# Order of the two score matmul pairs within a visit of a fused attention and feed-forward kernel

## What is computed

```python
xn   = layernorm(x)                                  # over the 256 channels
q, k, v = split(xn @ qkv_w + qkv_b)                  # 16 heads of 16 channels
attn = softmax(einsum('bnhd,bmhd->bhnm', q, k) * 0.25)
a    = einsum('bhnm,bmhd->bnhd', attn, v).reshape(b, n, c) @ proj_w + proj_b
h    = silu(xn @ (w_gate/127).T) * (xn @ (w_up/127).T)   # 768 wide
out  = x + a + h @ (w_down/127).T
```

## Time and profile before

| | us |
|---|---|
| three timed runs | 644.5, 646.66, 642.33 (median 644.5) |
| the profiled execution | 647.3 |
| its span in the profile | 645.2 |
| TensorE busy in the span | 608.5 (94%) |
| VectorE busy | 506.7 (79%) |
| ScalarE busy | 365.4 (57%) |
| GpSimd busy | 162.2 (25%) |

### The profile page before, as it was taken

One profiled execution on the slowest core, in us unless ns is written; L12 is line 12 of the kernel. 1 busy time (PEld: TensorE's weight loads), 2 busy tenths in 40 slices (PEclk: granted clock), 3 DMA queues, 4 the chain that ended last, 5 costly groups with the idle time before them and its releaser, 6 DMA issues.

```text
span 645.2 us, 10919 instructions
## 1 busy us (share of the span) xinstructions
PE 608.5 (94%) x3612; PEld 331.4 (51%) x3612; DVE 506.7 (79%) x693; ACT 365.4 (57%) x467; POOL 162.2 (25%) x165
## 2 busy tenths in 40 slices
PE   7888999999999989999899999999999999999885
PEld 6554455554545545554455545455455455554334
DVE  5897887887888887898878887888878877887712
ACT  3544655656565555665456564656556655656471
POOL 3124153121421224220531214211242202112110
PEclk9998999999999999999999999999999999999998
DMA  8760282117412282204622065112822046121101
GB/s 292 225 104 3 98 197 51 51 36 189 119 38 49 69 245 63 50 5 154 169 49 50 34 197 127 21 49 94 233 50 50 3 153 144 50 50 35 34 2 36
DMA packets 38075, 59.10 MB, mean 92 GB/s; under 512 B 5792, under 2 KB 21152, under 8 KB 38048
## 3 DMA queue, kind: packets, MB, share of 16 engines
q1 hardware_dynamic: 36896, 58.22, 33.4%
q10 hardware_dynamic: 1152, 0.52, 0.3%
HBM read 37.23 MB, written 20.97 MB: 90 GB/s over the span
## 4 chain that ended last, share of the span: by engine, by line
PE 72%; DVE 9%; issue 6%; DMA 6%; ACT 5%; POOL 1%; ACTq 0%; DVEq 0%; POOLq 0%
PE dense L891 31%; PE o_bank L881 16%; PE st_bank L850 13%; PE s_bank L867 9%; DMA q_stack<-max_tl 5%; DVE neg_max L656 4%; ACT probs L531 2%; PE dense L905 1%; PE dense L922 1%; ACT qk_parts L547 1%; DVE o_blocks L725 1%; POOL xn L460 1%; DVE stats L638 1%; DVE v_ones L684 1%; DVE inv_sum L729 0%
## 5 line engine op out<-in xcount | busy, mean ns | idle before, releaser
L531 ACT ACTIVATE probs<-st_bank 128x1024 f32<-128x1024 f32 x250 | 255.9, 1024 | 233.4 <-PE st_bank L850 229.5
L656 DVE TENSOR_REDUCE neg_max<-s_bank 128x2 f32<-128x1024 f32 x250 | 304.8, 1219 | 72.7 <-PE s_bank L867 70.0
L881 PE MATMUL o_bank<-probs,v_ones 128*32 128x512 f32 x1024 | 138.1, 612 | 6.9 <-ACT probs L531 3.8
L850 PE MATMUL st_bank<-q_stack,k_stack 50*128 50x512 f32 x500 | 125.0, 496 | 9.5 <-DMA q_stack<-max_tl 5.3
L468 POOL TENSOR_TENSOR hid_tl<-hid,hid_th 128x512 fp32r<-128x512 f32 x48 | 61.7, 1286 | 240.8 <-ACT hid_th L585 240.8
L867 PE MATMUL s_bank<-k_stack,q_stack 48*128 48x512 f32 x500 | 111.2, 441 | 4.5 <-DVE neg_max L656 3.6
L850 PEld LDWEIGHTS st_bank<-q_stack,k_stack 50*128 50x128 f32 x500 | 46.8, 184 | 125.3 <-ACT probs L531 82.7
L867 PEld LDWEIGHTS s_bank<-k_stack,q_stack 48*128 48x128 f32 x500 | 47.2, 185 | 30.7 <-DVE neg_max L656 29.2
L881 PEld LDWEIGHTS o_bank<-probs,v_ones 128*32 128x32 f32 x1024 | 20.3, 108 | 51.4 <-issue 46.1
L499 POOL TENSOR_TENSOR resid<-resid,p_bias 128x256 f32<-128x256 f32 x32 | 22.4, 730 | 96.9 <-DMA resid<-in_L_attn_x 96.9
L692 DVE SCALAR_TENSOR_TENSOR gated<-gated,dense 128x512 f32<-128x512 f32 x48 | 32.7, 681 | 13.5 <-ACT gated L559 12.3
(11 more groups left out here) (100 smaller groups left out, 684.0 us busy)
## 6 DMA issues: line engine op xcount, KB each, us to landing
q_spread<-qk_parts SPq DMA_DIRECT2D x16, 512.0 KB, 3.6
k_spread<-qk_parts SPq DMA_DIRECT2D x16, 512.0 KB, 3.3
q_stack<-q_spread SPq DMA_DIRECT2D x64, 128.0 KB, 3.1
k_stack<-k_spread SPq DMA_DIRECT2D x64, 128.0 KB, 3.3
q_stack<-q_spread SPq DMA_DIRECT2D x64, 64.0 KB, 3.3
k_stack<-k_spread SPq DMA_DIRECT2D x64, 64.0 KB, 3.2
resid<-in_L_attn_x SPq DMA_DIRECT2D x8, 512.0 KB, 5.0
xn<-in_L_attn_x SPq DMA_DIRECT2D x7, 512.0 KB, 3.5
```

What stands on the lines that cost most here:

```text
L531: nc.scalar.activation(probs[:, s % 2, 2 * half:2 * half + 2, :], transposed_bank(row, s, half)[:, :, :], ACT.Exp, scale=SCALE).then_inc(e ...
L656: nc.vector.tensor_reduce(neg_max[:, g % 2, :, NT * pair + qt], score_bank(row, half)[:, :, :], AX_X, ALU.max, negate=True).then_inc(max_d ...
L850: done = nc.tensor.matmul(transposed_bank(row, s, half)[:, r, :], k_stack[rows, pair, P * kt:P * (kt + 1)], q_stack[rows, pair, :], start= ...
L881: done = nc.tensor.matmul(o_bank[32 * j:32 * (j + 1), :], v_ones[:, kt, 8 * (g // 2) + 2 * j + g % 2, :], probs[:, (s - 1) % 2, j, :], sta ...
```

## The change

`pairs` calls `scores` before `scores_t`. Nothing else differs: the same instructions, waits and buffers, on every engine.

```diff
             def pairs(row, s, half):
+                if pair_ahead(row, s, half):
+                    scores(row, s, half)
                 if row.has(0):
                     scores_t(row, s, half)
-                if pair_ahead(row, s, half):
-                    scores(row, s, half)
```

## The result

| | us |
|---|---|
| kernel before, median of 4 runs | 644.11 (642.33 to 646.66) |
| changed kernel, median of 4 runs | 658.25 (656.33 to 658.9) |
| ratio, with its 95% interval | 1.0212 (1.017 to 1.0253) |
| profiled executions, before and after | 647.3 and 657.95 |
| their spans | 645.2 and 655.9 |

The changed kernel is 14.1 us slower by the medians.

A forecast was written before the change was run, and what follows sets the result against it. TensorE's queue was taken to set the end. Six sequences at 1.86 us (11.2), sequence 0 at 2.5 and sequence 7 at 0.3 gave +14.0 us, 658.5 against the median 644.5; 8 in 10 between 647 and 667.

The forecast's parts named there:

- steps 8 and 9: Around the maxima's DMA wait: idle time covers part of the loss, then step 9 stalls; 1.06 us in all after step 9.
- steps 13 to 15: VectorE's gate half, behind a later exponential and tanh, delays the reduction: about 0.27 us each, +0.8 a sequence.
- What bounds the kernel: Whole kernel: TensorE, busy 94%, sets the end by its queue; the change can only add or remove a few stalls.
- The unit: Two visits of one undisturbed step: TensorE free at 2.48 us instead of 2.49, so the same cost to 0.01 us.
- Price (a): Where a maxima pair's reduction end did not move, the waiting pair holds the transposed pair behind it: 0.22 to 0.23 us more.
- Price (b): Where ScalarE's work behind an exponential feeds VectorE and then a reduction, that reduction is late by 0.23 or 0.40 us.
- steps 3, 6 and 7: First pairs of these steps wait for reductions delayed by later exponentials: +0.46, +0.27 and +0.40 us a sequence.
- Step 1: The product with V waits less for VectorE's v, because the reduction of step 0 is early: -0.15 us.
- Sequences 0 and 7: First sequence, without a DMA wait to cover delays: 2.5 us; last, without chunks for a next one: +0.3 us.
- VectorE first pays: Rival: reductions 0.23 us sooner shrink TensorE's stalls at about 4 places a sequence; -7 us, 637; chance 0.09.
- Nothing measurable: Rival: shifts disappear in TensorE's idle time and the DMA wait; about 4.5 us slower, 649; chance 0.19.
- The worse one: Rival: later exponentials delay dense work by 0.1 us in another 4 steps a sequence; +3 to +5, 663; chance 0.16.

The follow-up runs named there:

- control trace: Kernel before with ScalarE's tanh of the gate ahead of its copy of the hidden activations at slot 2 of steps 12 to 15; ratio 1.001.

## Why the prediction was right

The forecast against the median was 658.5 and the median is 658.25; the working called for +14.0, the medians moved by 14.1. The agreement to 0.25 us is luck: the interval of the ratio alone reaches from 10.9 to 16.3 us, and the terms that were off, by about +2.2 us (steps 8 and 9) and -1.7 us (steps 13 to 15) over six sequences, nearly cancel. What was right is the mechanism and its size, 15.0 us by the steps against the control trace.

*What bounds the kernel.* Right. TensorE's queue set the end, VectorE was idle often enough not to, and an order that serves VectorE first only moved the waiting into TensorE.

*The unit.* Right to 0.01: 2.48 was worked out and measured, with the reduction at 0.54, the exponential at 0.78 and the pair at 1.82. The kernel with six steps exchanged shows that it is free in time as well (its only cost is at step 9).

*Price (a), 0.22 to 0.23.* Right: 0.67 against 0.44, and the kernel with only visit 1 exchanged, which pays it in twelve steps of sixteen, costs 3.4%.

*Price (b) at steps 3, 6 and 7.* Right: +0.49, +0.27, +0.41 against 0.46, 0.27, 0.40. The runs with these steps in the old order, and the one with the shorter ScalarE chain, take them away and leave the others.

*Steps 8 and 9.* Mis-sized: +0.08 was said, +0.36 measured in sequence 4. I let the DMA of the maxima decide when step 8 goes on, as it does in the earlier trace rows. In the changed kernel it mostly does not: in sequences 1, 2, 4 and 6 its first pair waits for VectorE's reduction (line 656), 0.28 us beyond TensorE's arrival (in sequence 2 its weight load waits 0.64 us, where a load that nothing holds up shows 0.36), and the transposed pair follows 0.34 behind it, with the DMA landed by then. In sequences 3 and 5 the transposed pair does wait for the DMA, 0.77 and 0.28 us. The kernel with steps 5 to 7 in the old order shows where the reduction's lateness comes from: it is gone there, and 0.2 us of step 8 with it. So the step that failed is the DMA as the end of the wait at step 8; a reduction made late by the steps ahead stood there in its place. The loss ahead was then not swallowed, and step 9 pays price (a) and the later exponential of step 8 together, +0.48. Against the control trace the two steps come, without the dips of the clock, to +0.45 in the mean of sequences 1 to 6, between +0.13 and +1.2, the highest where the DMA landed late.

```profile
234.50 1.22 DVE L656 TENSOR_REDUCE neg_max<-s_bank 128x2 f32<-128x1024 f32 x1
...
235.77 0.50 PE L867 MATMUL s_bank<-k_stack,q_stack 48*128 48x512 f32 x2 [0.21 <-DVE neg_max L656]
...
236.11 0.39 PE L850 MATMUL st_bank<-q_stack,k_stack 50*128 50x512 f32 x2
```

These are lines of the changed kernel's timeline, sequence 2, step 8: the releaser is the reduction, and no DMA stands in a bracket.

*Steps 13 to 15.* Mis-sized the other way: 0.8 was said, 0.51 measured. The mechanism is right (the tanh ahead of the copy removes exactly these). The gate's half came 0.30 later in the step and not 0.40, and the reduction starts 0.08 ahead of the end of the gate's row, where I had counted 0.04. The exponential itself came 0.37 later, and the tanh followed it after 1.45 (419.26 to 420.71) where it had been 1.51.

*Step 1.* -0.15 was said, -0.03 is left. The product with V starts earlier by 0.09 against its pair (1.13 behind the first pair of the visit, 203.79 - 202.66, where the earlier trace rows and its pair at 201.06 have 1.22), and not by 0.20, and the next visit returns most of that. The reduction ahead of v had no room to come 0.23 sooner: it stands behind VectorE's transpose of the attention output and starts 0.73 after its pair, at 201.11, and not 0.54.

*Sequences 0 and 7.* 2.5 and 0.3 were said; against the control trace they are 2.2 and 0.5. The gain of 0.12 a step in steps 5 to 8 of sequence 7 did not come: step 5 costs 0.13, the others 0.05 or less.

*Rivals.* VectorE first pays: its sign is refuted by the result, and its premise by the runs: where a reduction was late, ScalarE's queue was the reason at steps 3, 6, 7 and 13 to 15. The rule "Identifying the Most-Contended Engine" of the Trainium skill's "Perfetto Trace Analysis" would have pointed to VectorE's 79%. Its next section, "Optimization Strategy", asks which gaps stand on that engine, who ends them, and how that could start sooner; read so, the 70.0 us of VectorE waiting for TensorE invite the exchange. It did shorten that gap, to 40.9 us, and the kernel became 14.1 us slower: here the measurement goes against the rule. An engine that stands waiting 70.0 us for TensorE was not what set the pace. Nothing measurable: refuted. The worse one: no four further steps with 0.1 us each were found; steps 0, 2, 4, 5, 10, 11 and 12 moved by 0.03 or less in sequence 4.

## What to carry to other kernels

When an engine's queue feeds two readers from single buffers, the pair with the later release belongs behind the other one: a waiting instruction in first place holds the second, here for 0.23 us where nothing else waits, and the second reader starts later too. Before a reader is served first, follow what stands behind the *other* reader in its own queue; the exponential's 0.23 to 0.40 us came back through the tanh, the bias copies and the maxima copy as stalls of the engine that was to be helped. And a chain that ends in a stall is cheaper to shorten than to start earlier: moving one 0.6 us copy and one 0.4 us statistics gave -0.8%.

## What the runs showed of the hardware that was not expected

**The granted clock dips at places of its own.** Three stretches of the kernel before and two of the changed one (us, busy times, granted clock in the third column from the end):

```profile
46.00:54.00 8.00, 7.10 (x41) 5.12 (x43) 6.10 (x11) 3.62 (x5) 1.28 (x1) 0.79 0.01 2
597.00:599.00 2.00, 2.00 (x13) 0.59 (x5) 0.75 (x2) 0.27 (x1) 0.00 (x0) 0.50 0.73 248
628.00:633.00 5.00, 3.88 (x21) 1.06 (x22) 0.38 (x1) 1.89 (x2) 0.00 (x0) 0.74 0.01 3
```

```profile
241.00:248.00 7.00, 6.60 (x36) 3.91 (x40) 5.15 (x12) 2.38 (x3) 4.31 (x5) 0.76 0.60 122
320.00:330.00 10.00, 9.65 (x59) 5.86 (x58) 7.13 (x14) 4.77 (x6) 7.35 (x7) 0.83 0.41 81
```

At 0.50 TensorE runs at 1.2 GHz, and the stretches of 0.74 to 0.83 are part 1.2 and part 2.4. Against the control trace, which has no dip until its last microsecond, the three places of the kernel before are 1.5, 1.5 and 0.9 us longer. The two dips of the changed kernel, both from the end of step 9 into step 10, cost 1.5 and 1.4 us against the same steps in the kernel with the tanh ahead. With both sides corrected (3.8 off the one, 2.9 off the other) the profiled spans differ by 11.6 us and not 10.7. The kernel before also had late landings in its profiled execution: its step 8 is 0.6, 0.9 and 0.9 us longer than in the control trace in sequences 1, 2 and 3, and with these 2.4 us the difference is 14.0.

Before the first of the two dips of the changed kernel, TensorE had stood idle 1.10 us and 0.36 us for the reductions of step 9. That idle time alone does not bring a dip. Six traces of kernels with the new order in steps 8 to 15 are at hand; in all 36 of their sequences 1 to 6 TensorE stands idle 0.75 us or more at that place, and in six of them the clock dips behind it. In the four traces with the old order, where it stands idle 0.45 us or less there, none of 24 sequences has a dip at that place. So a dip now and then seems to be a further cost of the change, about 1.5 us each; what decides between the six and the thirty stays open.

**The same small DMA lands sooner or later.** In the kernel before, from the start of the DMA to the pair that waits for it, sequences 3 and 4:

```profile
302.75 0.52 ACTq L608 DMA_DIRECT2D q_stack<-max_th  x1
...
309.33 0.50 PE L850 MATMUL st_bank<-q_stack,k_stack 50*128 50x512 f32 x2 [1.48 <-DMA q_stack<-max_tl]
...
378.11 0.52 ACTq L608 DMA_DIRECT2D q_stack<-max_th  x1
...
383.56 0.50 PE L850 MATMUL st_bank<-q_stack,k_stack 50*128 50x512 f32 x2 [0.32 <-DMA q_stack<-max_tl]
```

6.58 and 5.45 us for the same transfer at the same place of a sequence, with the stacks' transfers in flight beside it. Where it is late, the step is up to 1.1 us longer. These two effects, a microsecond at a time, are a good part of why single executions of one kernel lie 4 to 9 us apart here: the scatter (standard deviation) of the kernel before was 2.2, 2.6 and 1.9 us beside the three groups of runs, and a straight line in the granted clock leaves 0.8, 1.6 and 1.1 us of it. They are also why the account by steps told more than the medians of small edits. What makes the one landing late was not tried.
